# A three-hop graph attention kernel: dense part as one block, finer relu signals, one predicated copy a sort step

## What is computed

```python
agg = h
for _ in range(3):
    hd = agg[head]; t = agg[tail]
    att = sum((hd @ q_w) * tanh(rel * t @ k_w), axis=1)
    e = exp(att - segment_max(att, head)[head])
    w = e / segment_sum(e, head)[head]
    agg = segment_sum(w[:, None] * rel * t, head) / max(count, 1)
    agg = agg / max(norm(agg), 1e-12)
    out = out + agg + h
result = x + out
```

## Time and profile before

| | |
|---|---|
| median of 3 runs | 2046.64 us (2031.48 to 2052.04) |
| the profiled execution | 2049.01 us |
| its span, first to last instruction | 2046.8 us |
| busy DVE, POOL, PE, ACT | 1364.2, 1234.4, 1100.0, 846.4 us |
| the sort's end, seen as POOL's first gather | 191.8 us |
| first scatter of hop 0 | 762.2 us |
| first gather of hop 1 | 1094.9 us |
| first gather of hop 2 | 1488.0 us |
| the mean granted TensorE clock | 0.688 |

### The profile page before, as it was taken

The page is one execution under the profiler, slowest core; times in us unless marked ns, Lnnn a source line. Parts: engine busy times, 40 slices in busy tenths (PEclk is TensorE's granted clock), DMA queues, the critical chain, the costliest instruction groups (busy, mean ns, idle before and its releaser), DMA issues. The chain is left out here.

```text
span 2046.8 us, 23618 instructions
## 1 busy us (share of the span) xinstructions
PE 1100.0 (54%) x5196; PEld 874.6 (43%) x5196; DVE 1364.2 (67%) x6127; ACT 846.4 (41%) x2649; POOL 1234.4 (60%) x1218
## 2 busy tenths in 40 slices
PE   0111354557669668732213588987646886856420
PEld 0001233336447446721212466776524665646320
DVE  8987588776675675778762348676713365789870
ACT  2221466666555554555541224544512143234420
POOL 1001776666777676774466777740077676767776
PEclk9999966665666675555555878886667697765555
DMA  8811655545433343354454555641299989757771
GB/s 228 239 47 51 219 178 182 177 150 179 123 92 112 96 124 99 130 173 164 164 165 137 151 145 157 189 126 64 91 159 146 130 167 178 161 157 212 213 207 34
DMA packets 199661, 302.94 MB, mean 148 GB/s; under 512 B 31696, under 2 KB 113948, under 8 KB 196064
## 3 DMA queue, kind: packets, MB, share of 16 engines
q1 hardware_dynamic: 161120, 228.46, 35.4%
q0 software_dynamic: 38400, 72.99, 19.3%
HBM read 175.89 MB, written 130.86 MB: 150 GB/s over the span
## 5 line engine op out<-in xcount | busy, mean ns | idle before, releaser
L1522 PE MATMUL ps<-rt,wr 128*125 128x128 f32 x1200 | 267.3, 393 | 240.2 <-DVE wr L1083 217.6
L638 POOL DMA_INDIRECT tr<-in_x_dram,tidx x200 | 204.0, 1020 | 286.1 <-DVEq L881 184.3
L1522 PEld LDWEIGHTS ps<-rt,wr 128*125 128x125 f32 x1200 | 232.0, 288 | 262.4 <-DVE wr L1083 236.0
L638 POOL DMA_INDIRECT tr<-agg_d,tidx x200 | 194.8, 974 | 204.5 <-issue 189.9
L1451 PE MATMUL ps<-ident,rt 128*128 128x128 f32 x600 | 137.2, 371 | 290.4 <-DVE rt L1145 226.9
L650 POOL DMA_INDIRECT ntab_d<-rt,lidx x200 | 211.1, 1055 | 115.4 <-issue 64.6
L1331 ACT ACTIVATE sqj<-ps,invc 125x128 bf16<-125x128 f32 x600 | 212.3, 371 | 158.9 <-PE ps L1522 158.9
L1290 ACT COPY rtT<-ps 128x512 f32<-128x512 f32 x150 | 88.0, 586 | 413.0 <-PE ps L1451 412.6
L1145 DVE TENSOR_TENSOR rt<-tr,relr 128x512 f32<-128x512 f32 x150 | 101.3, 688 | 229.6 <-ACT hr L1282 123.8
L650 POOL DMA_INDIRECT out_dram<-rt,lidx x200 | 212.2, 1061 | 69.8 <-issue 60.5
L638 POOL DMA_INDIRECT tr<-ntab_d,tidx x200 | 201.8, 1009 | 66.8 <-issue 66.8
(11 more groups left out here) (229 smaller groups left out, 2296.6 us busy)
## 6 DMA issues: line engine op xcount, KB each, us to landing
agg_d<-rt SPq DMA_DIRECT2D x100, 258.0 KB, 2.7
xr<-agg_d SPq DMA_DIRECT2D x100, 258.0 KB, 4.2
relr<-rel_d SPq DMA_DIRECT2D x100, 256.0 KB, 5.2
ntab_d<-rt SPq DMA_DIRECT2D x15, 1679.7 KB
rt<-in_x_dram SPq DMA_DIRECT2D x13, 1024.0 KB, 6.5
out_dram<-rt SPq DMA_DIRECT2D x13, 1024.0 KB, 4.1
acc_d<-xr SPq DMA_DIRECT2D x50, 258.0 KB, 3.5
rel_d<-relr SPq DMA_DIRECT2D x50, 256.0 KB, 3.8
```

Of the source, the lines that this page charges most:

```text
L638: G.indirect_dma_start(out=row, out_offset=None, in_=table[:, :], in_offset=bass.IndirectOffsetOnAxis(ap=idx[:, n:n + 1], axis=0)).then_in ...
L1522: ins = T.matmul(ps[B_T + j % 2][0:R, t, :], wr[:, (j % 2) * GT + t, 0:R], rt[:, j * GT + t, 0:D], start=True, stop=True)
```

## The change

Three things. In the sort, one predicated copy of 256 elements with a mask that is repeated for both halves takes the place of two of 128; its source is the whole old payload with its halves swapped, so ACT copies 256 elements to `vold`. In hop 0, ACT signals `s_lh` behind the four relus of `tr` and again behind the four of `hr` of each group, and DVE waits for each part by itself, product and base rows group by group. The dense part's remaining rows are done in 12 chunks of 16 rows a partition in one block behind hop 0's sums, from three buffers (`hr`, `relr`, and the tiles of the turned rows, now `turns`), with two sets of norms, and the relu goes to `xr`. The first three loads are issued ahead of the last chunk's sums; the first loads of hop 1 wait for all stores of the block.

```diff
-DC = 8
-TAIL = 4
+DC = 16
+DX = 3
...
+        turns = sb("turns", [P, 4 * GT, D])
+        rtT, thT = turns[:, 0:2 * GT, :], turns[:, 2 * GT:4 * GT, :]
...
+        dlns = [ln[:, :, 0:DC] for ln in lns]
...
+        vold = flat[:, 6 * SC:7 * SC]
...
-        xd = [hr[:, w * DC:(w + 1) * DC, :] for w in range(2)]
-        hd = ohT[:, :, :].rearrange("p u (t f) -> p (u t) f", f=D)
+        xd = [hr[:, :, :], relr[:, :, :], turns[:, :, :]]
+        hd = xr[:, 0:DC, 0:D]
+        spare = ohT[:, :, :].rearrange("p u (t f) -> p (u t) f", f=D)
...
-        dense_at = {}
-        chunks = iter(range(ND))
-        for j in range(NG - ND, NG - TAIL):
-            dense_at["sums", 0, j] = next(chunks)
-        for k in range(TAIL):
-            dense_at["tail", 0, k] = next(chunks)
...
             for h in range(HOPS):
                 if h > 0:
                     sp.wait_ge(s_cs, 16 * NG * h)
+                    for u in range(DX):
+                        sp.wait_ge(s_od[u], 16 * len(range(u, ND, DX)))
 
                     def load_rel(g):
                         if g < NG:
@@ -591,7 +565,8 @@
                     for r in range(TS):
                         sp.wait_ge(s_as[r], 16 * slot_total(r, TS))
                     sp.wait_ge(s_att, NG)
-                    load_x(0)
+                    for c in range(DX):
+                        load_x(c)
...
                     for g in range(NG - LAG, NG):
                         store_agg(h, g)
                     if h == 0:
-                        for k in range(TAIL):
-                            dense("tail", 0, k)
-                        store_out(ND - 1)
+                        for c in range(ND):
+                            store_out(c)
+                            load_x(c + DX)
...
+            for u in range(DX):
+                pool_wait(s_od[u], 16 * len(range(u, ND, DX)))
...
             def dense_in(c):
-                dve.wait_ge(s_xd[c % 2], 16 * (c // 2 + 1))
+                dve.wait_ge(s_xd[c % DX], 16 * (c // DX + 1))
                 for t in range(DC):
-                    ch.note(V.bn_stats(dstats[:, t, :], xd[c % 2][:, t, :]))
+                    ch.note(V.bn_stats(dstats[:, t, :], xd[c % DX][:, t, :]))
                 ch.join()
-                layer_norm(dstats, dlns, DC, s_dln)
+                layer_norm(dstats, dlns[c % 2], DC, s_dln)
 
             def dense_out(c):
                 dve.wait_ge(s_dh, c + 1)
-                V.scalar_tensor_tensor(flat2(xd[c % 2]), flat2(hd), 3.0, flat2(xd[c % 2]), ALU.mult, ALU.add).then_inc(s_do, 1)
-
-            def dense(what, h, s):
-                c = dense_at.get((what, h, s))
-                if c is not None:
-                    if c > 0:
-                        dense_out(c - 1)
-                    dense_in(c)
+                V.scalar_tensor_tensor(xd[c % DX], hd, 3.0, xd[c % DX], ALU.mult, ALU.add).then_inc(s_do, 1)
...
+                step = step_of[k, m]
                 gt = bank(2 + step % 2)[:, 0:128].rearrange("p (n s) -> p n s", s=stride)
-                old = vold.rearrange("p (n s) -> p n s", s=stride)
+                new, old = (t.rearrange("p (n t s) -> p n t s", t=2, s=stride) for t in (v, vold))
                 ch.note(V.tensor_tensor(gt, ka, kb, ALU.is_gt))
                 ch.note(V.tensor_tensor(na, ka, kb, ALU.min))
                 ch.note(V.tensor_tensor(nb, ka, kb, ALU.max))
                 dve.wait_ge(s_vc, step + 1)
                 dve.wait_ge(s_dve, ch.at - 2)
-                V.copy_predicated(va, gt.bitcast(I32), vb).then_inc(s_vx, 1)
-                dve.wait_ge(s_vx, n + 1)
-                V.copy_predicated(vb, gt.bitcast(I32), old).then_inc(s_vx, 1)
+                V.copy_predicated(new, gt.bitcast(I32).unsqueeze(2).to_broadcast([P, 128 // stride, 2, stride]),
+                                  old[:, :, ::-1, :]).then_inc(s_vx, 1)
                 ch.join()
...
-                dense("sums", h, j)
...
+                    dve.wait_ge(s_lh, 2 * g + 1)
...
+                dve.wait_ge(s_lh, 2 * g + 2)
...
-                        if old:
-                            dve.wait_ge(s_lh, s)
                         for g in old:
                             product(0, g)
-                        for g in old:
                             base_rows(g)
...
                 if h == 0:
-                    for k in range(TAIL):
-                        dense("tail", 0, k)
+                    for c in range(ND):
+                        dense_in(c)
+                        if c > 0:
+                            dense_out(c - 1)
                     dense_out(ND - 1)
...
+            for step, (k, m) in enumerate(SORT):
+                v = vT if m > 7 else vbuf
                 if k > 8 and m in (k - 1, 7):
                     turns += 1
                     act.wait_ge(s_xv, turns)
                     A.copy(v, bank(1)[:, 0:SC]).then_inc(s_vl, 1)
                     act.wait_ge(s_vl, turns)
-                elif n > 0:
-                    act.wait_ge(s_vx, n)
-                stride = 1 << (m - low)
-                A.copy(vold.rearrange("p (n s) -> p n s", s=stride),
-                       v.rearrange("p (n t s) -> p n t s", t=2, s=stride)[:, :, 0, :]).then_inc(s_vc, 1)
+                elif step > 0:
+                    act.wait_ge(s_vx, step)
+                A.copy(vold, v).then_inc(s_vc, 1)
...
-                relu_rows(dlns, 0, xd[c % 2], hd, DC).then_inc(s_dh, 1)
-
-            def dense_in(what, h, s):
-                if (what, h, s) in dense_at:
-                    dense(dense_at[what, h, s])
+                relu_rows(dlns[c % 2], 0, xd[c % DX], hd, DC).then_inc(s_dh, 1)
...
                             for i, g in enumerate(unit):
-                                relu_rows(lns[s % 2], i * GT, ring(tr, g, TS), ring(tr, g, TS), GT)
-                                ins = relu_rows(lns[s % 2], (2 + i) * GT, ring(xr, g, TS), ring(hr, g, RS), GT)
-                            ins.then_inc(s_lh, 1)
+                                relu_rows(lns[s % 2], i * GT, ring(tr, g, TS), ring(tr, g, TS), GT).then_inc(s_lh, 1)
+                                relu_rows(lns[s % 2], (2 + i) * GT, ring(xr, g, TS), ring(hr, g, RS), GT).then_inc(s_lh, 1)
...
                 if h == 0:
-                    for k in range(TAIL):
-                        dense_in("tail", 0, k)
+                    for c in range(ND):
+                        dense(c)
...
-                    pe.wait_ge(s_vx, payload_at[i + 9, i + 8 if way == 0 else 7][1])
+                    pe.wait_ge(s_vx, step_of[i + 9, i + 8 if way == 0 else 7])
```

More of the change, by code:

```diff
@@ L279, in gnn_kernel @@
         zeros = upper[0:ZP, 0:ZR]
-        xd = [hr[:, w * DC:(w + 1) * DC, :] for w in range(2)]
-        hd = ohT[:, :, :].rearrange("p u (t f) -> p (u t) f", f=D)
+        xd = [hr[:, :, :], relr[:, :, :], turns[:, :, :]]
+        hd = xr[:, 0:DC, 0:D]
+        spare = ohT[:, :, :].rearrange("p u (t f) -> p (u t) f", f=D)
         base_in = [hr[:, w * GT:(w + 1) * GT, :] for w in range(2)]
         one_in = [hr[:, (2 + w) * GT:(3 + w) * GT, :] for w in range(2)]
-        two_in = [hd[:, w * GT:(w + 1) * GT, :] for w in range(2)]
+        two_in = [spare[:, w * GT:(w + 1) * GT, :] for w in range(2)]
         ps = [ctx.enter_context(nc.psum_tensor(f"ps{i}", [P, GT, D], F32)) for i in range(8)]
@@ L361, in gnn_kernel @@
         s_sc = [sem(f"s_sc{r}") for r in range(RS)]
-        s_xd = [sem(f"s_xd{u}") for u in range(2)]
-        s_od = [sem(f"s_od{u}") for u in range(2)]
+        s_xd = [sem(f"s_xd{u}") for u in range(DX)]
+        s_od = [sem(f"s_od{u}") for u in range(DX)]
         s_dln = sem("s_dln")
@@ L372, in gnn_kernel @@
         s_pace = sem("s_pace")
[L375 to L384, removed]
+        SORT = [(k, m) for k in range(1, LOGN + 1) for m in range(k - 1, -1, -1)]
+        step_of = {km: i for i, km in enumerate(SORT)}
         block = ctx.enter_context(nc.Block())
@@ L501, in store_out @@
                 if c == ND - 1:
[L502 to L510 removed]
+                    sp.wait_ge(s_od[(c - 1) % DX], 16 * ((c - 1) // DX + 1))
+                sp.dma_start(dense_rows(out, c), xd[c % DX]).then_inc(s_od[c % DX], 16)
             def carries(h, b):
@@ L517, in load_last @@
             def load_last(g):
-                if g == 0:
-                    for u in range(2):
-                        sp.wait_ge(s_od[u], 16 * len(range(u, ND, 2)))
                 if g >= 2:
@@ L691, in _ @@
                     fetch(tr[:, (g % TS) * GT + t, :], g * GT + t, agg_d[1], tidx, s_t[g % TS])
-            for u in range(2):
-                pool_wait(s_od[u], 16 * len(range(u, ND, 2)))
+            for u in range(DX):
+                pool_wait(s_od[u], 16 * len(range(u, ND, DX)))
             for u in range(XE):
@@ L1266, in _ @@
             turns = 0
-            for step, (k, m, n) in enumerate(SORT):
-                v, low = (vT, 8) if m > 7 else (vbuf, 0)
+            for step, (k, m) in enumerate(SORT):
```

(2 more changed lines are left out.)

24 lines of the change are left out of this document (5 added, 19 removed).

## The result

The changed kernel takes 1962.6 us (median of four executions, 1960.3 to 1974.5) against 2041.4 us before (four, 2031.5 to 2052.0). The ratio is 0.963, with a 95% interval of 0.958 to 0.968: 79 us less, where 1954 was predicted. The profiled execution after took 1960.7 us (span 1958.8), at a mean granted TensorE clock of 0.70; the one before 2049.0 (0.69).

The account below looks back on a forecast made before the run. The prediction took DVE to bound the sort, DVE with ACT early hop 0, and DVE's dense chunks to set POOL's end in the sums; 2049.0 − 33 − 14 − 48 = 1954 us, forecast 1940 to 1968, range 1930 to 1996.

Parts of the forecast that it names:

- Part A: Sort: one predicated copy of 256 elements a step replaces two of 128, saving 33 us.
- slow form: Sort: predicated copy taking 0.43 us instead of 0.29 with partners 2 or 1 apart; the new copy was taken to have none.
- Part B: Hop 0: relu signalled twice a group, saving 1.2 us in each of about 12 steps with early chunks, 14 us.
- I give it nothing: Hop 0's later steps: a faster DVE finds the same loop of PE and ACT, so no gain was counted.
- Part C: Hop 0's sums: without dense chunks among them, POOL's waits for DVE vanish, saving 48 us up to hop 1.
- The block: Dense chunks behind hop 0's sums: starting at 933 us, 12 chunks at 9.8 us each, last output at 1056.
- Dense late (1): Rival: dense chunks take 11.5 to 12.5 us, transfers and scatters sharing queues; about 1973 us, chance 0.14.
- (2): Rival: sort barely faster, the new copies having the slow form; 1966 to 1986 us, chance 0.14.
- (3): Rival: hop 0's relu signals do nothing, PE and ACT being the loop; 1968 us, chance 0.09.
- (4): Rival: slower than before, dense block delaying hop 1's first product; decided at 19 us chunks, 2070 us at 21; chance 0.03.

Follow-up runs that it names:

- in company: The changed kernel with the twice-signalled relu of hop 0 taken back, set against the changed kernel: 1976.8 us, ratio 0.967 to the kernel before.
- C alone: The kernel before with only the dense part moved into 12 chunks of 16 rows behind hop 0's sums: 2009.4 us, ratio 0.984.
- B alone: The kernel before with only hop 0's relu signalled twice a group, product and base rows in turn: 2038.9 us, ratio 0.999.

## Why the prediction was right, and where it wasn't

The time, 1962.6, is 9 us above the forecast and inside both ranges. Part of that is the base: the sum started from an execution of 2049.0, and the median of before is 2041.4. Against like, 95 us were predicted and 79 came (88 between the two profiled executions).

- **Part A**, 33 us predicted, 32.2 in the trace and 34 (1.5%) in time. Right in its steps: copy 0.43 to 0.44 us (0.43 predicted), step 0.93 (0.94), ACT 0.405 (0.40), no slow form. Steps at distance 1 saved 0.46 us, as predicted, but those at distance 2 only 0.38: the sum gave all near steps the 0.09 by which a compare was longer before (0.38 instead of 0.29), and only the steps at distance 1 had it. The reason given for the absence of a slow form, that only pieces under 16 bytes in the target are slow, was wrong; the count of units touched is what the runs fit. The rule of the Trainium skill that the prediction named (Vector Engine (DVE) Microarchitecture Reference, 5.2, access granule), too, would have had a target in runs of two at full rate (0.44 measured) and the swapped source at distance 1 slow (not seen: 0.435, as at the other distances).
- **Part B**, 14 us predicted; about 10 by the ratios in company, 2 alone, and 5.5 that the traces show. The step that failed is its place. "There the loop of DVE and ACT is the bound" was read from DVE's wait of 1.2 us. A short wait for ACT's last relu says that DVE is nearly as slow as ACT, not that ACT waits for DVE; in the early steps ACT waited for PE alone, before and after. The prediction's own sign of being wrong, early steps still at 24 us, came true (23.9). And "I give it nothing" for the later steps is where the gain came from: 5.5 us in units 14 to 17. What the ratios hold beyond that is not shown by any trace. As far as the size came out near, it was by luck. B also has a cost that the sum had at nothing: in the kernels that have B whole the 400 gathers of hop 0 took 40 to 43 us more than 0.94 each, against 29 to 31 in the four without it. POOL waits 22 us besides in hop 0 of the changed kernel, so how much of those 10 us reached the time isn't known.
- **Part C**, 48 us predicted, 38 measured in the kernel with C alone (42 between the two profiled executions). POOL's waits for DVE did vanish (44.1 us to 3.7). The step that failed is the silent one, that a scatter takes as long beside the block as before: 13 us more for the 200. The gathers beside the 13 early outputs had shown it in the trace of before. 4 us of it came back in the wait ahead of hop 1's first gather, 6.17 to 2.25, which I had left unchanged.
- **The block**: pace 9.2 us (9.8 predicted; loads land in 5.2 to 6.0 us, not 6.5); with a sixteenth of the transfers 8.73, where 8.7 was worked out for DVE and ACT. Its first statistics are at 875.3, which is 919 in the times of before (43.3 us were gained ahead of the first scatter) and not 933; which of the terms was too large wasn't taken apart. The last output ends at 991.8, ahead of POOL's last scatter, and nothing of the block reached the path but by DVE's hold on POOL.
- **Rivals.** Dense late (1) did not happen, but its cost did, by another way: it had loads and stores slow each other, and what was slow was POOL. (2) didn't happen. (3) was right on the early steps; units 14 to 17 speak against the rest of it, while the time of B alone can't tell it from nothing. (4) decided at chunks of 19 us; they took 9.2.

Still open: how much of B lies beneath the clock in units 18 to 24, why that clock differs between kernels whose hop 0 is the same code, and what units 16 and 17 gain by: early products and an early base did the same there, and no run takes both apart from all that DVE does behind them.

## What to carry to other kernels

Ask of a loop between engines who waits for whom from both sides: that DVE waits for ACT makes no loop of the two unless ACT somewhere waits for DVE. When long DVE instructions are moved beside POOL's gathers or scatters, price POOL's durations and not only its waits (here the trace of before already had gathers of 2.0 to 3.0 us beside them), and keep one input of such an instruction in PSUM where a bank is free. Where an edit's gain sits in a stretch whose clock varies, compare unit by unit and not by the total alone.

## What the runs showed of the hardware

- A scatter issued by POOL while DVE runs an instruction with two SBUF inputs ends 0.8 to 0.9 us behind it (up to 3.07 us instead of 0.98), with one input in PSUM it isn't touched; 12 outputs of 2.28 us cost POOL 17 us. Gathers do the same (before: 2.0 to 3.0 us instead of 0.94 at 13 outputs).
- A predicated copy on DVE costs 4.4 ns for each 16-byte unit of the target touched (0.30, 0.44, 0.72 us for 128 elements over 32, 64, 128 units), on top of about 0.16 us, an estimate from the same three times. Hopping data cost nothing at 1 of 2 (0.302) and 0.075 us at 1 of 4 (0.377). In the changed kernel a plain compare, minimum or maximum of 128 elements takes 0.28 to 0.30 us at every distance.
- Two kernels with the same code in hop 0, at the same place of their executions, ran 25 and 64 matmuls in 8 us, at a granted clock of 0.50 and 0.96.
